# Cross-attention and expert FFN: Wk and Wv loaded and used by halves, context on ScalarE's queue, head-mixing loads behind Wv, means of Wq on two engines

## The reference

```python
# attention over the context, H = 16 heads of D = 64, on layernorm(x) without gain
q = einsum('bqc,chd->bqhd', layernorm(x), Wq) / sqrt(D)
k = einsum('bkc,chd->bkhd', ctx, Wk);  v = einsum('bkc,chd->bkhd', ctx, Wv)
attn = einsum('bqhd,bkhd->bhqk', q, k)
attn = softmax(einsum('bhqk,hi->biqk', attn, Wth1))      # heads mixed before ...
attn = einsum('bhqk,hi->biqk', attn, Wth2)               # ... and after the softmax
x = x + einsum('bqhd,hdc->bqc', einsum('bhqk,bkhd->bqhd', attn, v), Wo)
# FFN: each of 8 experts takes the 256 best of the tokens still left, by a score
# from layernorm and centroids; then layernorm, w1, gelu, w2, biases, residual
```

## Time and profile before

| what | value |
|---|---|
| median of 3 runs | 331.15 us |
| lowest, highest | 330.31, 333.5 us |
| profiled execution: time, span | 330.23 us, 328.1 us |
| TensorE matmuls busy | 287.9 us (88%) |
| VectorE busy | 218.3 us (67%) |
| ScalarE busy | 145.0 us (44%) |
| GpSimd busy | 178.0 us (54%) |
| mean granted clock of TensorE | 0.959 of full speed |

### The profile page before, as it was taken

The page is one execution under the profiler, slowest core; times in us unless marked ns, Lnnn a source line. Parts: engine busy times, 40 slices in busy tenths (PEclk is TensorE's granted clock), DMA queues, the critical chain, the costliest instruction groups (busy, mean ns, idle before and its releaser), DMA issues.

```text
span 328.1 us, 6528 instructions
## 1 busy us (share of the span) xinstructions
PE 287.9 (88%) x2080; PEld 252.8 (77%) x2081; DVE 218.3 (67%) x749; ACT 145.0 (44%) x265; POOL 178.0 (54%) x240
## 2 busy tenths in 40 slices
PE   7999998999999999998722579989999999889990
PEld 3999888999999999998711258878788788788990
DVE  0679999888788788877467887867777776120100
ACT  1366565465454556544430245353535253353420
POOL 8100444555665655555410677585868688877611
PEclk9999999999999999999955599999999999999998
DMA  7992006910010000011100042272728282916000
GB/s 263 357 381 88 2 0 215 391 68 35 37 59 32 32 32 32 32 44 55 64 32 0 16 178 56 73 266 64 284 57 294 54 290 61 332 31 197 36 16 16
DMA packets 21623, 37.50 MB, mean 114 GB/s; under 512 B 2400, under 2 KB 14944, under 8 KB 21216
## 3 DMA queue, kind: packets, MB, share of 16 engines
q1 hardware_dynamic: 19040, 30.89, 26.3%
q0 software_dynamic: 2560, 6.31, 6.3%
HBM read 30.90 MB, written 6.29 MB: 113 GB/s over the span
## 4 chain that ended last, share of the span: by engine, by line
PE 61%; DVE 14%; POOL 8%; DMA 8%; issue 6%; ACT 1%; SPq 0%; DVEq 0%; POOLq 0%; ACTq 0%
PE pair L892 51%; DMA G<-rows_scratch,idx 7%; PE pair L975 4%; POOL out_dram L445 4%; POOL w1p L424 3%; DVE cmpb L755 3%; PE pair L942 2%; DVE pair L788 2%; DMA wk_s<-wk_dram 2%; PE pair L1081 2%; POOL Htk L405 1%; PE pair L1047 1%; PE pair L1004 1%; DVE ok L775 1%; DVE Hoh L847 1%
## 5 line engine op out<-in xcount | busy, mean ns | idle before, releaser
L892 PE MATMUL pair<-w2s,hT 128*128 128x256 f32 x256 | 61.2, 384 | 0.0
L370 POOL TENSOR_TENSOR pr<-pr,rs 128x1024 f32<-128x1024 f32 x16 | 31.7, 1979 | 41.9 <-DVE rs L696 41.9
L892 PE MATMUL pair<-yT,w1p 128*128 128x256 f32 x384 | 52.6, 289 | 0.0
L892 PE MATMUL pair<-Bm,pT 128*128 (+1 forms) x384 | 50.0, 285 | 2.3 <-DVE pT L689 2.3
L892 PEld LDWEIGHTS pair<-w2s,hT 128*128 128x128 f32 x256 | 45.8, 190 | 4.8
L892 PEld LDWEIGHTS pair<-Bm,pT 128*128 128x128 f32 x384 | 47.0, 188 | 2.7 <-issue 2.7
L892 PE MATMUL pair<-Am,xTp 128*128 (+1 forms) x192 | 48.8, 402 | 0.0
L892 PEld LDWEIGHTS pair<-yT,w1p 128*128 128x128 f32 x384 | 47.8, 189 | 0.4
L569 ACT ACTIVATE hT<-pair,b1s 128x256 f32<-128x256 f32 x64 | 26.9, 471 | 44.0 <-PE pair L892 39.9
L892 PEld LDWEIGHTS pair<-Am,xTp 128*128 128x128 f32 x192 | 35.0, 188 | 7.3
L424 POOL TENSOR_TENSOR w1p<-w1s,w1p 128x512 fp32r<-128x512 f32 x32 | 40.1, 1276 | 0.2
(11 more groups left out here) (131 smaller groups left out, 527.7 us busy)
## 6 DMA issues: line engine op xcount, KB each, us to landing
w1s<-w_dram SPq DMA_DIRECT2D x8, 1024.0 KB
w2s<-w_dram SPq DMA_DIRECT2D x8, 1024.0 KB
rows_scratch<-row SPq DMA_DIRECT2D x16, 256.0 KB, 2.0
xs<-x_dram SPq DMA_DIRECT2D x1, 2048.0 KB, 17.1
xTs<-xT_dram SPq DMA_DIRECT2D x1, 2048.0 KB, 18.8
wk_s<-wk_dram SPq DMA_DIRECT2D x1, 1024.0 KB, 5.2
wv_s<-wv_dram SPq DMA_DIRECT2D x1, 1024.0 KB, 7.4
wqT_s<-wqT_dram SPq DMA_DIRECT2D x2, 512.0 KB, 8.9
```

What stands on the lines that cost most here:

```text
L370: pool_mul = nc.gpsimd.tensor_tensor(p4, p4, rs[:, v, :].unsqueeze(1).unsqueeze(3).to_broadcast([P, KG, H, K8]), ALU.mult)
L892: return nc.tensor.matmul(out_, l, r, start=start, stop=stop)
```

## The change

Wk and Wv are loaded in two halves each, 512 of the 1024 columns at a time, in the order of use, and TensorE waits for each half by itself. The context is issued on ScalarE's queue. GpSimd issues the 16 head-mixing loads only once the second half of Wv has landed; its two memsets go ahead of them. VectorE makes the mask behind fill 19 in place of fill 5. The first half of Wq (blocks 0 to 3) is summed, scaled and centred by VectorE alone, now ahead of its fill 1; of the second half ScalarE takes the means by four accumulating passes, whose other output goes to `xTp` and is not used, and centres blocks 6 and 7, while VectorE centres 4 and 5. TensorE runs 6 warm-up matmuls in place of 12.

```diff
--- before.py
+++ after.py
@@ -33,7 +33,7 @@
 BASE_BITS = 0x4B000000
 LO = 16
 EPS = 1e-5
-WARM, BUSY = 12, 3
+WARM, BUSY = 6, 3
 TAKEN = -3.0e38
 
 
@@ -153,11 +153,11 @@
             yTs = sb("yTs", [P, 2, C], f32, tiles)
         w1p = sb("w1p", [P, 2, 2, CC, F], f32r)
 
-        s_in = {n: sem("in_" + n) for n in ("cst", "ctx", "wk", "wv", "wq0", "wq1", "wo", "rep", "small", "x", "xT", "b2")}
+        s_in = {n: sem("in_" + n) for n in ("cst", "ctx", "wk0", "wk1", "wv0", "wv1", "wq0", "wq1", "wo", "rep", "small", "x", "xT", "b2")}
         s_consts, s_ones, s_mix = sem("consts_made"), sem("ones_made"), sem("mix_made")
         s_fill, s_evA, s_evD = sem("bank_filled"), sem("filled_copied_act"), sem("filled_copied_dve")
         s_bn1, s_mv1, s_ve1, s_r1 = sem("x_stats"), sem("x_mean_var"), sem("x_var_eps"), sem("x_rstd")
-        s_wm, s_wcA, s_wcD = sem("wq_mean"), sem("wq_centred_act"), sem("wq_centred_dve")
+        s_wm, s_wmA, s_wcA, s_wcD = sem("wq_mean"), sem("wq_mean_act"), sem("wq_centred_act"), sem("wq_centred_dve")
         s_xTh, s_xTs = sem("xT_high"), sem("xT_rest")
         s_gc, s_gm, s_cent = sem("gain_centroids"), sem("their_means"), sem("centred_centroids")
         s_lg, s_mx, s_sub, s_exp = sem("logits_made"), sem("max_made"), sem("max_subtracted"), sem("exp_made")
@@ -292,9 +292,10 @@
         @block.sync
         def _(sp):
 
-            sp.dma_start(ctx_s[:], ctxT.rearrange("(c p) n -> p c n", p=P)).then_inc(s_in["ctx"], 16)
-            sp.dma_start(wk_s[:], wk.rearrange("(c p) n -> p c n", p=P)).then_inc(s_in["wk"], 16)
-            sp.dma_start(wv_s[:], wv.rearrange("(c p) n -> p c n", p=P)).then_inc(s_in["wv"], 16)
+            for to, w, name in ((wk_s, wk, "wk"), (wv_s, wv, "wv")):
+                for h in range(2):
+                    half = slice(h * HD // 2, (h + 1) * HD // 2)
+                    sp.dma_start(to[:, :, half], w.rearrange("(c p) n -> p c n", p=P)[:, :, half]).then_inc(s_in[f"{name}{h}"], 16)
             for h in range(2):
                 sp.dma_start(wqT_s[:, 4 * h:4 * h + 4, :],
                              wqT.rearrange("(j p) n -> p j n", p=P)[:, 4 * h:4 * h + 4, :]).then_inc(s_in[f"wq{h}"], 16)
@@ -334,11 +335,13 @@
         @block.gpsimd
         def _(pool):
 
+            nc.gpsimd.memset(mhalf[:], -0.5).then_inc(s_consts, 1)
+            nc.gpsimd.memset(inv_c[:], 1.0 / C).then_inc(s_consts, 1)
+
+            pool.wait_ge(s_in["wv1"], 16)
             for o, src in ((0, wth1), (1, wth2T)):
                 for k in range(K8):
                     pool.dma_start(wrep[k:P:K8, o, :], src).then_inc(s_in["rep"], 16)
-            nc.gpsimd.memset(mhalf[:], -0.5).then_inc(s_consts, 1)
-            nc.gpsimd.memset(inv_c[:], 1.0 / C).then_inc(s_consts, 1)
             pool.wait_ge(s_consts, 2)
             pool.wait_ge(s_in["xT"], 16)
 
@@ -475,16 +478,21 @@
                 nc.scalar.activation(xTp[:, 0, v, :].rearrange("p (c n) -> p c n", c=CC), xTs[:, :, ds(t * P, P)],
                                      ACT.Copy).then_inc(s_xTh, 1)
 
-            def centre(h):
-
-                act.wait_ge(s_wm, 2 * h + 2)
-                for j in (4 * h + 2, 4 * h + 3):
+            act.dma_start(ctx_s[:], ctxT.rearrange("(c p) n -> p c n", p=P)).then_inc(s_in["ctx"], 16)
+
+            def centre_second():
+
+                act.wait_ge(s_in["wq1"], 16)
+                for j in range(4, 8):
+                    nc.scalar.activation(xTp[:, j // 2 % 2, j % 2, :], wqT_s[:, j, :], ACT.Copy, scale=-1.0 / C,
+                                         accum_out=wneg[:, j:j + 1]).then_inc(s_wmA, 1)
+                for j in (6, 7):
+                    act.wait_ge(s_wmA, j - 3)
                     nc.scalar.activation(wqT_s[:, j, :], wqT_s[:, j, :], ACT.Identity, bias=wneg[:, j:j + 1]).then_inc(s_wcA, 1)
 
             for f in range(LATE):
                 if f == 2:
-                    centre(0)
-                    centre(1)
+                    centre_second()
                 if f == 20:
                     act.wait_ge(s_in["cst"], 16)
                     nc.scalar.activation(exp_r[:], expand, ACT.Copy).then_inc(r_init, 1)
@@ -598,16 +606,24 @@
                 dve.wait_ge(s_evA, MIXED // 2 + f - MIXED + 1)
                 nc.vector.tensor_tensor(mixed(f, 1), fill_bank(f)[:], mixed(f, 0).bitcast(f32), ALU.subtract).then_inc(s_evD, 1)
 
-            def centre(h):
-
-                q = slice(4 * h, 4 * h + 4)
-                dve.wait_ge(s_in[f"wq{h}"], 16)
-                nc.vector.tensor_reduce(wneg[:, q], wqT_s[:, q, :], AX.X, ALU.add).then_inc(s_wm, 1)
-                dve.wait_ge(s_wm, 2 * h + 1)
-                nc.vector.tensor_scalar(wneg[:, q], wneg[:, q], -1.0 / C, None, ALU.mult).then_inc(s_wm, 1)
-                dve.wait_ge(s_wm, 2 * h + 2)
-                for j in (4 * h, 4 * h + 1):
-                    nc.vector.tensor_scalar(wqT_s[:, j, :], wqT_s[:, j, :], wneg[:, j:j + 1], None, ALU.add).then_inc(s_wcD, 1)
+            def centred(j):
+                nc.vector.tensor_scalar(wqT_s[:, j, :], wqT_s[:, j, :], wneg[:, j:j + 1], None, ALU.add).then_inc(s_wcD, 1)
+
+            def centre_first():
+
+                dve.wait_ge(s_in["wq0"], 16)
+                nc.vector.tensor_reduce(wneg[:, 0:4], wqT_s[:, 0:4, :], AX.X, ALU.add).then_inc(s_wm, 1)
+                dve.wait_ge(s_wm, 1)
+                nc.vector.tensor_scalar(wneg[:, 0:4], wneg[:, 0:4], -1.0 / C, None, ALU.mult).then_inc(s_wm, 1)
+                dve.wait_ge(s_wm, 2)
+                for j in range(4):
+                    centred(j)
+
+            def centre_second():
+
+                for j in (4, 5):
+                    dve.wait_ge(s_wmA, j - 3)
+                    centred(j)
 
             def x_stats(t):
 
@@ -627,13 +643,14 @@
                 if f >= MIXED:
                     mixed_rest(f)
                 elif f % 2 == 1:
+                    if f == 1:
+                        centre_first()
                     dve.wait_ge(s_fill, f + 1)
                     copy_fill(f, lambda to, src, scale: nc.vector.tensor_scalar(to, src, scale, None, ALU.mult)).then_inc(s_evD, 1)
 
                 if f == 1:
-                    centre(0)
-                    centre(1)
-                if f == 5:
+                    centre_second()
+                if f == 19:
 
                     dve.wait_ge(s_in["cst"], 16)
                     dve.wait_ge(s_in["rep"], 16 * 2 * K8)
@@ -906,8 +923,8 @@
             f = 0
 
             for w, name in ((wk_s, "wk"), (wv_s, "wv")):
-                pe.wait_ge(s_in[name], 16)
                 for g in range(2):
+                    pe.wait_ge(s_in[f"{name}{g}"], 16)
                     for j in range(4):
                         for c in range(CC):
                             last = mm(bank[f][:, j * P:(j + 1) * P], w[:, c, (4 * g + j) * P:(4 * g + j + 1) * P],
@@ -923,9 +940,11 @@
                     if f >= 8:
                         wait_copied(pe, f - 5)
                     for m in range(HD // P):
-                        if side == 0 and c == 0 and m % 4 == 0:
-                            pe.wait_ge(s_wcA, m // 2 + 2)
-                            pe.wait_ge(s_wcD, m // 2 + 2)
+                        if side == 0 and c == 0 and m == 0:
+                            pe.wait_ge(s_wcD, 4)
+                        if side == 0 and c == 0 and m == 4:
+                            pe.wait_ge(s_wcD, 6)
+                            pe.wait_ge(s_wcA, 2)
                         for o in range(2):
                             q = slice(o * D, (o + 1) * D)
                             last = mm(bank[(f + m // 4 * 2 + o) % 8][:, m % 4 * P:(m % 4 + 1) * P],
```

## The result

The changed kernel is 0.5% slower: median 332.19 us of 22 runs against 330.92 of 22 for the kernel before, ratio 1.005 with a 95% interval of 1.0031 to 1.0068. One of the 22 executions of the kernel before took 881.82 us; the ratios in this document are of fast executions alone, so they leave it out and can differ a little from the quotient of two medians. The forecast was a small gain (330.5 us against a median of 331.15, a profiled execution 0.4 us shorter, ratio 0.999).

The account below looks back on a forecast made before the run. TensorE and VectorE were both taken as full from 22.54 to 43.65 us, VectorE's sequence setting the end. 0.86 less 0.61 plus 0.15 slack saves 0.40: 330.23 to 329.8, plus 0.7 for the median, 330.5 us; range 329.0 to 332.8.

Parts of the forecast that it names:

- the rival of the late clock: Preamble, TensorE: with fewer warm-up matmuls it stays at 1.2 GHz to 11 us, giving 332.1 us; chance 0.08.
- The step that failed: Preamble loads: shorter runs of Wk and Wv lose 0.1 us, so Wq's halves land at 10.15 and 11.75 us.
- its bound: Landing of Wq's first half: forecast at 10.15 us, with bounds 10.05 and 10.75.
- Wk's head start: Preamble, TensorE: Wk by halves and context on ScalarE's queue start Wk near 5.1 us; Wv ends 1.5 us sooner.
- the next wait, for Wq: TensorE after Wv: ready at 12.4 us, it waits for VectorE's kvT copy until 13.35; 0.5 of 1.5 us is left.
- The mask's loads: Head-mixing loads behind Wv: land at 22.3 us, hidden by 0.7; rival, slower issues, VectorE waits 6.4 us, 336.9 us, chance 0.05.
- The mask behind fill 19: VectorE before the first ABT copy: the mask adds 0.61 us, less 0.15 of slack.
- The stall that its going from fill 5 ends: TensorE before Wo at 18.66 us: its 0.31 us idle, ended by a VectorE copy, goes.
- ScalarE's passes: Second half of Wq: four accumulating passes at 0.54 us, 2.15 in all; its matmuls start at 14.85 in place of 15.40.
- up to 0.9 us of lateness is free: Late clock, TensorE before Wq: lateness up to 0.9 us costs nothing, as TensorE waits for 13.35 us anyway.
- keeping the rise where it was: Warm-up of six matmuls ending at 4.0 us: the sum left the clock's rise to 2.4 GHz at about 4.3 us.

Follow-up runs that it names:

- halves_only: The kernel before with only Wk and Wv loaded and waited for by halves of 512 columns, all on SyncE's queue; ratio 1.0050 to the kernel before.
- halves_by_rows: The kernel before with Wk and Wv each loaded in two transfers cut by input channels, keeping runs of 4 KB; ratio 0.9997 to the kernel before.
- warm_12: The changed kernel with 12 warm-up matmuls in place of 6; ratio 1.0041 to the kernel before.
- after_whole: The changed kernel with Wk and Wv loaded and waited for whole again, still 6 warm-up matmuls; ratio 1.0045 to the kernel before.

## Why the prediction was wrong

Take T apart by three stretches. To Wq's start: forecast 0.5 us sooner, measured 2.16 later. From there to Wo's end: forecast 0.35 sooner, measured 1.23 sooner. From there to T: forecast 0.46 later, measured 1.18 later. 2.16 - 1.23 + 1.18 = 2.11, the whole of it. That the measured 332.19 us lies inside the range, by the 332.1 of the rival of the late clock, is luck: the clock was late, but what TensorE waited for was Wq.

- **The step that failed** is "Wk and Wv in runs of 2 KB lie between: 0 to 0.7 us lost. I take 0.1". Cut by columns, the loads brought Wq's first half at 12.65 us, 2.5 later than the forecast and 1.9 beyond its bound. Two things were wrong in it. The rate did not lie between the two of the rows, 353 and 401 GB/s, but below both, 299 and 320 from 6 to 8 us. And a mean rate is not enough, since the DMA engines drift apart and a transfer lands with the last of them. halves_only shows the step by itself, with Wq's first half at 12.05, at 1.1 us of T and 0.5% of time; halves_by_rows shows that cutting by rows is free.
- **Wk's head start** came in part: 5.52 us for 5.1, because the context landed only at 5.44. I had argued that the next wait, for Wq, takes all but 0.5 us of it. It took the rest too, and 2.16 more: the kind was right, the meeting point lay far later.
- **The mask's loads** came late, the rival in kind. Its stated reason was wrong: GpSimd's issues took 0.48 to 0.52 us each in the median beside VectorE's additions, no more than the 0.52 to 0.53 alone. The Trainium skill's rule that `tensor_scalar` in a mode using both ports blocks GpSimd ("SBUF — State Buffer", section "Who interferes with whom") found no case here: four additions of 256 elements took 1.14 us, still about one nanosecond an element. The loads were late because Wv was, 11.2 in place of 8.7, and the last took 6.3 us to land where I had taken 5.6. Price 0.84 us against the forecast of none.
- **The mask behind fill 19** was nearly right: 0.36 for 0.46. The stall that its going from fill 5 ends was under-priced: I took the 0.31 of noted idle time, and it was worth 0.58.
- **ScalarE's passes** cost 0.40 us each with the accumulator read, where I took 0.54; the step was right in kind, and its gain in the stretch from Wq's start to Wo's end was 0.65 where the noted idle time was 0.37.
- **The clock** rose late, the other rival: Wk's matmuls took 5.33 us. I wrote that up to 0.9 us of lateness is free; with Wq landing late, more was. Hidden here, it is the second full cause behind the first: taking away one alone brings little back (1.0041 in warm_12, 1.0045 in after_whole), taking away both brings 0.999. I went wrong in keeping the rise where it was. I took from one execution that it comes at 4.3 us; under the same twelve matmuls it came after 6.1 in four others. Six end at 4.20, and then the pace stayed that of 1.2 GHz until between 8 and 9 us. That TensorE had idled 0.98 us without losing its clock did not bear on this: there it had risen before the pause, here it had not.

Open: why the cut by columns slows the stream, and how much of the later landing (12.65 against 12.05) is due to the context's own queue; what sets when the clock rises under the same warm-up.

## What to carry to other kernels

Splitting a load to start sooner pays only if what is waited for next does not come later; follow the queue to the next landing, not to the first, and cut by rows, not by columns, until it has been measured. An idle gap closed between matmuls can be worth more than its noted length (0.58 us for 0.31 here), since neighbours then overlap. Let a warm-up last until the first operand lands, since the moment at which the clock rises varies. Where two waits end at about the same time, undo them together in a test, or each will look innocent.

## What the runs showed of the hardware

- Matrices with rows of 4 KB, loaded as halves of 512 columns, moved at 232 to 328 GB/s from 6 to 8 us in seven kernels; loaded by whole rows, at 378 to 426 in ten, also when cut in two by rows.
- DMA engines drift apart under one queue: in the changed kernel 50 packets of the constants had moved by 12.0 us, and the transfer two places ahead of them landed at 12.65.
- A transfer of 128 KB on a second queue landed 4.6 to 5.9 us after its issue beside transfers of 512 KB and 1 MB; at the head of the one queue it took 2.1 to 2.3.
- ScalarE's pass with an accumulator output repeats every 0.40 us for 256 elements, the read of 0.19 included.
- GpSimd issued small transfers every 0.48 to 0.53 us in the median, with VectorE idle or busy.
- Twelve warm-up matmuls of 512 columns took 4.11 us in one execution and 5.30 in others: the clock's rise came at about 4.3 us or not before 6.1. Before the first rise the profile's granted clock reads 1.00 also where the pace is that of the lower level.
- An idle stretch of 1.86 us on TensorE ahead of Wq was followed by a fall to 1.2 GHz in one execution, and pauses of 1.6 in others were not.
